# The second attention rewritten: fp16 hi/lo probabilities as the stationary operand

## The reference

```python
xn = layernorm(x, ln_x_g, ln_x_b)          # x is the context, 256 rows a batch
ln = layernorm(latents, ln_l_g, ln_l_b)    # latents: the layer-normed tokens, 256 rows
q = (ln @ Wq).reshape(b, m, h, d).transpose(0, 2, 1, 3)
kv = jnp.concatenate([xn @ Wkv, ln @ Wkv], axis=1)
...
qn = rmsnorm(q, qn_g) * scale
kn = rmsnorm(k, kn_g)
sim = jnp.einsum('bhid,bhjd->bhij', qn, kn)
sim = jnp.where(padded_mask[:, None, None, :], sim, max_neg)
attn = jax.nn.softmax(sim.astype(jnp.float32), axis=-1).astype(sim.dtype)
out = jnp.einsum('bhij,bhjd->bhid', attn, v)
return out @ Wout + bout
```

## Time and profile before

| | |
|---|---|
| median of 3 runs | 1444.24 us (1442.98 to 1446.23) |
| the profiled execution's own time | 1436.58 us |
| its span in the profile | 1434.8 us |
| TensorE busy, all of the span | 1091.6 us (76%) |
| VectorE | 1061.0 us (74%) |
| ScalarE | 789.7 us (55%) |
| GpSimd | 442.0 us (31%) |
| mean granted TensorE clock | 0.893 |

### The profile page before, as it was taken

One profiled execution on the slowest core, in us unless ns is written; L12 is line 12 of the kernel. 1 busy time (PEld: TensorE's weight loads), 2 busy tenths in 40 slices (PEclk: granted clock), 3 DMA queues, 4 the chain that ended last, 5 costly groups with the idle time before them and its releaser, 6 DMA issues. The chain is left out here.

```text
span 1434.8 us, 23644 instructions
## 1 busy us (share of the span) xinstructions
PE 1091.6 (76%) x7405; PEld 710.0 (49%) x7410; DVE 1061.0 (74%) x1847; ACT 789.7 (55%) x1340; POOL 442.0 (31%) x410
## 2 busy tenths in 40 slices
PE   1378888437999414899989899898989989936737
PEld 0245555313444202466666566565656666733426
DVE  8478888675666687777888788888778888646941
ACT  2246666623545324677777677776777676632112
POOL 7001010024777305322333321333312333001135
PEclk9789999767999755899999999999999999967969
DMA  4302010000000200000000000000000000050040
GB/s 183 90 4 25 13 24 0 25 12 12 22 22 16 92 0 1 1 1 1 1 1 0 0 0 0 0 0 0 0 0 0 0 0 1 1 201 1 14 134 27
DMA packets 22587, 33.22 MB, mean 23 GB/s; under 512 B 3856, under 2 KB 19711, under 8 KB 21446
## 3 DMA queue, kind: packets, MB, share of 16 engines
q1 hardware_dynamic: 21096, 29.74, 7.1%
q0 software_dynamic: 1440, 2.82, 0.6%
HBM read 26.52 MB, written 8.77 MB: 25 GB/s over the span
## 5 line engine op out<-in xcount | busy, mean ns | idle before, releaser
L1430 PE MATMUL e_mix<-e_probs,e_v_ones 128*128 128x256 f32 x1024 | 280.9, 394 | 3.8 <-ACT e_mixed L1499 2.4
L1291 POOL TENSOR_TENSOR e_raw<-e_raw,e_inv 128x512 f32<-128x512 f32 x96 | 115.0, 1205 | 384.8 <-DVE e_inv L1557 384.8
L1430 PEld LDWEIGHTS e_mix<-e_probs,e_v_ones 128*128 128x128 f32 x1024 | 179.9, 194 | 45.5 <-issue 25.2
L1574 DVE TENSOR_REDUCE e_row_max<-e_row_scores 128x1 f32<-128x512 f32 x256 | 165.6, 680 | 16.3 <-PE e_row_scores L1359 15.9
L1522 ACT ACTIVATE e_probs<-e_scores 128x512 f32<-128x512 f32 x256 | 142.2, 599 | 26.3 <-PE e_scores L1418 25.1
L1299 POOL TENSOR_TENSOR e_natural<-e_raw,e_natural 128x512 f16<-128x512 f32 x96 | 114.7, 1194 | 60.1 <-DVE e_natural L1568 60.1
L1359 PE MATMUL e_row_scores<-e_k_high,e_q_high 65*128 65x512 f16 x256 | 90.6, 388 | 55.0 <-DVE e_row_max L1574 50.0
L1418 PE MATMUL e_scores<-e_q_high,e_k_high 128*128 128x256 f16 x512 | 129.2, 285 | 0.0
L1417 PE MATMUL e_scores<-e_q_stack,e_k_stack 128*128 128x256 f16 x512 | 128.6, 285 | 0.0
L1614 DVE RECIPROCAL e_inverse<-e_summed 128x256 f32<-128x256 f32 x64 | 111.7, 1746 | 7.4 <-ACT e_mixed L1499 7.2
L1542 DVE TENSOR_REDUCE e_sum_sq<-e_squares 128x8 f32<-128x512 f32 x96 | 65.7, 685 | 62.3 <-ACT e_squares L1470 61.0
(11 more groups left out here) (361 smaller groups left out, 2597.6 us busy)
## 6 DMA issues: line engine op xcount, KB each, us to landing
w<-in_w SPq DMA_DIRECT2D x2, 2048.0 KB, 10.0
c_w<-in_w SPq DMA_DIRECT2D x17, 192.0 KB, 2.4
placed_scratch<-in_no_rows SPq DMA_DIRECT2D x1, 2313.0 KB, 16.2
...
a_mask_k<-in_mask_k SPq DMA_DIRECT2D x1, 2048.0 KB, 14.7
parts_scratch<-a_parts SPq DMA_DIRECT2D x2, 1024.0 KB, 4.0
...
```

The lines of the kernel that those rows point to most:

```text
L1291: nc.gpsimd.tensor_tensor(raw[:, j], raw[:, j], bc(inv[:, HU * j:HU * j + HU], (P, HU, D1), 2), ALU.mult).then_inc(normed, 1)
L1430: mm = pe.matmul(mix[:, 0:S], v_ones[par][:, kt, h, :], probs[buf][:, kt, :], start=(kt == 0), stop=(kt == KT - 1))
L1574: dve.tensor_reduce(row_max[:, i, qt:qt + 1], row_scores[qt][:], AX.X, ALU.max).then_inc(max_done, 1)
```

## The change

`attend_layer1` and its plan are rewritten; all else is as it was.

- **Weighing.** ScalarE forms the exponentials of a head twice, in fp32 (`probs`) and in fp16 (`p_hi`), 128x1024 each. VectorE subtracts them to `p_lo` (event `lo`): head 0's at the end of its step, head 1's early in the next. `p_hi` and `p_lo` are the stationary operands. The moving one is `v_cols`, per head 130 fp16 columns: v's high part, a one, v's low part. A head has 24 products (2 query blocks x 4 key blocks x 3) of 65, 64 and 65 columns, and the result has queries on the partitions, with the sum in column 64 of each.
- **Scaling** reads PSUM: a reciprocal of 128x4 and one product a pair of heads (event `n`), with no copy by ScalarE. The attended pair is transposed (event `a`) and copied by ScalarE for the Wout projection, which stands in step p=2 of the even units.
- **v** is copied by ScalarE as its fp16 high part and VectorE forms its low part from the misc bank, which is free only after that.
- **Maxima.** The maximum is negated in the same instruction; one transpose turns the four columns, ScalarE copies 4x128, and a DMA of SyncE puts them in `q_high`. `k_high` and `q_high` are filled by six DMAs a unit (64x8x128 fp16 each) in place of VectorE's copies.
- **PSUM.** The row scores have one bank, so that each product waits for the maximum before it; the scores of each head have two banks.
- **Order.** The blocks' jobs are spread otherwise: projections of k and q for the unit after next are spread over p=0 to 3 (k3, q0, q1 in p=3), v over p=0 and p=1, the transposes over p=1 and p=2, and the root stands at the end of p=3, in place of p=0's twelfth place. `raw` is double.

The core of the diff:

```diff
-JOBS = [[("q", t) for t in range(QT)] + [("v", t) for t in range(3)],
-        [("v", t) for t in range(3, KT)] + [("tk", t) for t in range(2)],
-        [("tk", t) for t in range(2, KT)] + [("tq", t) for t in range(QT)],
-        [("k", t) for t in range(KT)]]
-SPLITS = [[("root",)], [("split", j) for j in range(4)], [("split", j) for j in range(4, 6)], []]
-ROOT_AT = 12
...
+KQ = [("k", t) for t in range(KT)] + [("q", t) for t in range(QT)]
+VALUES = [[0, 1, 2], [3], [], []]
+TURNS = [[], [("tk", 0), ("tk", 1)], [("tk", 2), ("tk", 3), ("tq", 0), ("tq", 1)], []]
+RAWS = [KQ[0:1], KQ[1:2], KQ[2:3], KQ[3:6]]
+SPLITS = [[0, 1], [2, 3], [4, 5], []]
...
+    jobs = early + (turns[:2] + raws + values + turns[2:])
...
+    if p < PU - 1:
+        out = n0[:1] + r[0] + w[0] + lo1 + job(0) + r[1] + n0[1:2] + job(1) + [("s", 0)] + n0[2:] + r[2] + n1[:1] \
+            + w[1] + job(2) + r[3] + n + n1[1:2] + job(3) + m + n1[2:] + job(4) + [("s", 1)] + [("lo", 0)] + job(5) + job(6) + job(7)
...
+        out = w[0] + lo1 + job(0) + [("s", 0)] + r[0] + job(1) + w[1] + r[1] + job(2) + r[2] + n + job(3) + r[3] + job(4) + m \
+            + [("s", 1)] + [("lo", 0)] + job(5) + job(6) + job(7) + ([("root",)] if project else [])
...
-        v_ones = [sb(f"v_ones{i}", [P, KT, HU, P], F32) for i in range(2)]
...
+        v_cols = [sb(f"v_cols{i}", [P, KT, HU, VC1], F16) for i in range(2)]
...
+        row_scores = psum("row_scores", [P, NK1])
+        scores = [psum(f"scores{i}", [P, KT, S]) for i in range(2)]
+        mix = psum("mix", [P, 2, S])
         misc = [psum(f"misc{i}", [P, 512]) for i in range(2)]
...
+                if name == "tk":
+                    dma = sp.dma_start(k_high[par][0:D1, :, cols], k_stack[par][0:D1, :, cols])
...
+                    dma = sp.dma_start(q_high[par][0:D1, :, cols], q_stack[par][D1:P, :, cols])
...
+                row = q_high[par][MROW1:MROW1 + 1, 2 * p:2 * p + 2, :].rearrange("o h (t c) -> o (h t) c", c=P)
+                sp.dma_start(row, neg_rows[p % 2][:]).then_inc(max_in, 16)
...
+                pe.transpose(bank[0:2 * QT, 0:P], neg_max[buf][:], ident32[:]).then_inc(ready, 1)
...
+            def rows(q, par, p, i, qt):
...
+                    pe.wait_ge(max_done, n)
...
+            def weigh(q, i, par, p):
+                pe.wait_ge(lo_done[i], q + 1)
+                if not (isinstance(q, int) and q == 0):
+                    pe.wait_ge(att_done, q)
+                h = 2 * p + i
+                for qt in range(QT):
+                    at = slice(P * qt, P * qt + P)
+                    out = mix[:, i, (D1 + 1) * qt:(D1 + 1) * (qt + 1)]
+                    for kt in range(KT):
+                        values = v_cols[par][:, kt, h, :]
+                        first, last = qt == 0 and kt == 0, kt == KT - 1
+                        pe.matmul(out, p_hi[i][:, kt, at], values[:, 0:D1 + 1], start=first, stop=False, skip_group_check=True)
+                        pe.matmul(out[:, 0:D1], p_hi[i][:, kt, at], values[:, D1 + 1:2 * D1 + 1], start=False, stop=False, skip_group_check=True)
+                        mm = pe.matmul(out, p_lo[i][:, kt, at], values[:, 0:D1 + 1], start=False, stop=last, skip_group_check=True)
+                mm.then_inc(weighed, 1)
...
-                mm = pe.matmul(mix[:, 0:S], v_ones[par][:, kt, h, :], probs[buf][:, kt, :], start=(kt == 0), stop=(kt == KT - 1))
...
+                act.activation(squares[j % 2][:], heads(bank), ACT.Square).then_inc(taken, 1)
...
+                act.copy(v_cols[par][:, event[1], :, 0:D1], heads(bank)).then_inc(v_high, 1)
...
+                act.copy(stack[:, :, P * t:P * t + P].bitcast(F32), bank[:].rearrange("p (h t) -> p h t", h=HU)).then_inc(taken, 1)
...
+                act.copy(neg_rows[buf][:], bank[0:2 * QT, 0:P]).then_inc(taken, 1)
...
-                act.copy(summed[buf][at, :], mix[D1:P, 0:S])
-                act.copy(mixed[buf][at, :], mix[0:D1, 0:S]).then_inc(mix_taken, 1)
...
-                            act.activation(probs[i][:, 2 * half:2 * half + 2, :], scores[(2 * i + half) % 3][:], ACT.Exp).then_inc(exp_done, 1)
...
+                                act.wait_ge(lo_done[i], q)
                                 act.wait_ge(weighed, 2 * q + i - 1)
-                            act.activation(probs[i][:, 2 * half:2 * half + 2, :], scores[(2 * i + half) % 3][:], ACT.Exp).then_inc(exp_done, 1)
-                        elif name == "w" and rest[1] == KT - 1:
...
-                dve.tensor_scalar(neg_max[:, :, MROW1], row_max[:].rearrange("p i t -> p (i t)"), -1.0, None, ALU.mult).then_inc(neg_done, 1)
...
+            def low_values(event, use, u, par):
+                bank, n = use
+                dve.wait_ge(v_high, KT * u + event[1] + 1)
+                cols = v_cols[par][:, event[1], :, :]
+                dve.tensor_tensor(cols[:, :, D1 + 1:2 * D1 + 1], misc[bank][:].rearrange("p (h d) -> p h d", h=HU), cols[:, :, 0:D1],
+                                  ALU.subtract).then_inc(misc_taken[bank], 1)
...
+                dve.tensor_reduce(neg_max[buf][:, 2 * i + qt:2 * i + qt + 1], row_scores[:], AX.X, ALU.max, negate=True).then_inc(max_done, 1)
...
+            def low_probs(q, i):
+                dve.wait_ge(exp_done, 2 * (2 * q + i + 1))
+                dve.tensor_tensor(p_lo[i][:], probs[i][:], p_hi[i][:], ALU.subtract).then_inc(lo_done[i], 1)
...
-                dve.reciprocal(inverse[:], summed[buf][:]).then_inc(inverted, 1)
...
+                dve.reciprocal(inverse[:], mixed[:, :, :, D1]).then_inc(inverted, 1)
...
+                dve.tensor_tensor(out, mixed[:, :, :, 0:D1], bc(inverse[:], (P, 2, QT, D1), 3), ALU.mult).then_inc(att_done, 1)
```

More of the change, by code:

```diff
@@ L1124 @@
-MISC = ("k", "q", "v", "tk", "tq", "o", "m")
-START = [("k", t) for t in range(KT)] + [("q", t) for t in range(QT)] + [("root",)] + [("v", t) for t in range(KT)] \
-    + [("split", j) for j in range(6)] + [("tk", t) for t in range(KT)] + [("tq", t) for t in range(QT)] \
-    + [("r", i, qt) for i in range(2) for qt in range(QT)] + [("neg",), ("m",)] + [("k", t) for t in range(KT)]
+    hf, p = divmod(s, PU)
+    produce, project = not (last and hf), not last
+    ahead, behind = not (last and s == 2 * PU - 1), not (first and s == 0)
@@ new lines, in plan_step @@
+    norms = [[("norm", j), ("hi", j), ("low", j)] for j in SPLITS[p]] if produce else []
+    early = [("o",)] if s == 2 and not first else []
+    early += [("a",)] if not (first and s < 2) else []
+    raws = RAWS[p] if project else []
+    values = [("v", t) for t in VALUES[p]] if produce else []
+    turns = TURNS[p] if produce else []
+    jobs = early + (turns[:2] + raws + values + turns[2:])
+    w = [[("w", i)] if behind else [] for i in range(2)]
+    r = [[("r", i, qt)] if ahead else [] for i in range(2) for qt in range(QT)]
@@ L1164, in __init__ @@
         self.b, self.first, self.last = b, first, last
-        self.bank = FIRST_BANK if first else 0
-        start = totals(START, 0)
+        start = totals(START)
         if first:
@@ L1246, in attend_layer1 @@
+        lo_done = [sem(f"lo_done{i}") for i in range(2)]
         UB = 2
@@ L1344, in turn, with turn_max @@
                 mm.then_inc(ready, 1)
[L1346 removed]
+            def turn_max(use, q, buf):
                 bank, ready = emptied(use)
[L1348 to L1360 removed]
@@ new lines, in turn_attended, with project @@
+            def turn_attended(use, q, buf):
+                bank, ready = emptied(use)
+                pe.wait_ge(att_done, q + 1)
+                for qt in range(QT):
+                    mm = pe.transpose(bank[:, P * qt:P * qt + P], attended[buf][:, qt, :], ident32[:])
+                mm.then_inc(ready, 1)
+            def project(use, turned):
+                bank, ready = emptied(use)
+                pe.wait_ge(misc_taken[turned[0]], turned[1] + 1)
+                for qt in range(QT):
+                    for pair in range(H1 // 2):
+                        mm = pe.matmul(bank[:, P * qt:P * qt + P], attended_t[:, pair, P * qt:P * qt + P], keep["wout"][:, pair, :],
+                                       start=(pair == 0), stop=(pair == H1 // 2 - 1))
+                mm.then_inc(ready, 1)
@@ L1414, in batch @@
-                            for kt in range(2):
-                                out = scores[(2 * i + half) % 3][:, kt, :]
-                                cols = slice(P * (2 * half + kt), P * (2 * half + kt) + P)
-                                pe.matmul(out, k_stack[hf][:, h, cols], q_stack[hf][:, h, :], start=True, stop=False)
-                                mm = pe.matmul(out, k_high[hf][:, h, cols], q_high[hf][:, h, :], start=False, stop=True)
+                            if i == 0:
+                                pe.wait_ge(max_in, 16 * (q + 1))
@@ new lines, in batch @@
+                            if not (bt.first and s == 0):
+                                pe.wait_ge(exp_done, 2 * (2 * q + i - 1))
+                            for kt in range(KT):
```

(13 more changed lines are left out.)

523 lines of the change are left out of this document (252 added, 271 removed).

## The result

The changed kernel takes 1548.79 us, the median of four runs (1543.88 to 1560.61), against 1443.61 of the kernel before (1441.71 to 1446.23): the ratio is 1.0739, with a 95% interval of 1.067 to 1.0809. It is slower by 105 us. The forecast of slower held, the range (1405 to 1580) holds the time, and the 1512 was short by 37. In the four runs a longer time goes with a lower mean clock, from 1543.88 us at 0.859 to 1560.61 at 0.846.

The account below looks back on a forecast made before the run. TensorE (0.907 busy) and VectorE (0.82) feed each other in strict order, neither full. +4.3 us a unit over 14.7 units (+63) plus 5 at the ends gives 1504.6 profiled, 1512 as median; range 1405 to 1580.

Parts of the forecast that it names:

- VectorE's work: VectorE in a unit of eight heads: 12.5 us removed, 13.0 added, so 36.1 us of work against 35.6.
- the 2.2 us before the first row score: Step p=3: VectorE stands 2.2 us because all row scores wait for the DMA of q_high, taken at 2.4 us.
- v2 behind v1's bank: Step p=0: v2's projection needs the misc bank that v1 holds until VectorE's low part, and runs to 25.1 us.
- Weighing: TensorE's 24 fp16 products a head, taken at 30 ns each, 0.72 us a head in place of 2.2.
- Rival D: Stationary loads pace the weighing's products: 2.33 us a head, +12.9 us a unit, 1700 us or so; chance 0.04.
- high price of 76 ns: Upper bound for one weighing product on TensorE, from eight 128x128 products in 0.61 us; gave the range's upper end, about 1580.
- the clock, 0.5 us a unit: TensorE idles longer, so its granted clock falls under 0.96; 0.5 us a unit added, bounds 0 and 2.5.
- the walk: Row durations put on a unit's new order: p=3 13.35 us, p=0 12.6, p=1 and p=2 9.75 each; sum 45.45.
- case E: TensorE's gaps grow, its clock falls to the lower level for part of each step: 2 to 2.5 us a unit, 1541; chance 0.11.
- my sum: A unit of 47.7 us against 43.4: +4.3 over 14.7 units, +63 us, and 5 us for the stage's start and end.
- The stage's ends: Start and end of the second attention: 5 us added for a single row bank, DMA waits and two more q projections.
- Rival B: Faster: work lines up and VectorE is full, idling under 7.3 us a unit; a unit takes 39.8 us, 1396; chance 0.22.

Follow-up runs that it names:

- q_no_vlow: The changed kernel without v's low part: the second weighing product takes v's high part and ScalarE's copy frees the bank; 1486.20 us, ratio 1.0316.

## Why the prediction was right, and where it was short

- **Direction: right, for the reason given.** VectorE's work was forecast to stay (36.1 a unit, measured 34.6) and its idle to grow (7.8 to 11.6, measured 14.9). Long steps p=3 and p=0, the 2.2 us before the first row score, the DMA's 2.4 us (the median is 2.6), and v2 behind v1's bank are all in the trace.
- **Weighing: right.** 30 ns taken, 31 measured. Rival D falls. The Trainium skill, "TensorE: Matmul & The Clock Gate", section "LDWEIGHTS (loading the stationary operand)", prices one load of 128 columns, and the load records here (103 to 106 ns) agree with its figure; but the loads start 31 ns apart with their products, so that length is not the price of a product in this weighing. The high price of 76 ns was misread: the eight transposes of the earlier trace rows lie 56 ns apart (the next product starts 0.45 us after the first of them), and the last record's length was counted in. So the upper end of the range rested on a price that was too high.
- **The mis-sized term: the clock, 0.5 us a unit.** At the full clock the walk's p=3 holds (13.48 measured, 13.35 walked), so I take what that step lasts beyond it, 15.2 on the mean, as the clock's: 1.7 us, and 2.3 in the unit shown. In p=0 the lower clock costs 1.8 (13.35 against 11.58). That makes some 3.5 us a unit, an estimate from these steps, above my bound of 2.5, and about half of the 105 us if all units are alike. TensorE's busy time points the same way: 6.9 us a step forecast, 8.9 measured (463.21 / 52), and in p=3 7.87 at the full clock against 10.22 at 0.79. My case E had the mechanism, and its 1541 is the nearest number; but its sign, a clock under 0.85, did not come (0.90 in the stage).
- **Luck.** The walk gave p=0 12.6 us, and the step measured at 0.93 takes 11.58. That 1.0 too much paid for a third of the clock's missing 3.0, so that the unit of 49.5 us lies only 1.8 above the 47.7 of my sum. ScalarE's 6.9 to 7.0 us a step don't follow from the earlier trace rows, which give 7.8; the sum didn't use them. The low parts took 1.29 us, over the 1.1 to 1.25 that I had named.
- **The stage's ends: 5 us taken, 25 measured**, with the other 79 in the 13 periods (my sum had 63 for 14.7). I scaled by units, but the last two, with few or no projections, also got slower, some 44 us each against 35; that it is the low parts and scores, which stay in them, was not tested.
- **Rival B** failed at its condition: VectorE would have had to idle under 7.3 us, and idles 14.9.
- **What stays open.** Undoing single pieces gives 57 (low parts), 63 (v's low parts), 25 (row bank) and 23 (order), together more than the 105, while the savings of the change (reciprocals, TensorE's 1.5 us a head) must be paid from the same account. Each piece also moves the clock (in `q_no_vlow` four steps p=3 have 0.99 or 1.00, in the changed kernel none), so the clock's half is not a piece beside these, and no share of the loss belongs to one of them alone. What makes the clock fall at one wait and not at the next stays open, as does the one wait of 4.6 us for nothing that the profile shows.
